# Delta rule, chunk stage: the folding's sums on TensorE instead of VectorE

## The reference, cut to what matters

```python
def step(S, inp):
    qt, kt, vt, at, bt = inp
    v_hat = jnp.einsum('bij,bi->bj', S, kt)
    err = vt - v_hat
    S = at[:, None, None] * S + bt[:, None, None] * (kt[:, :, None] * err[:, None, :])
    o = jnp.einsum('bij,bi->bj', S, qt)
    return (S, o)
_, O = lax.scan(step, S0, (Q.swapaxes(0, 1), Kh.swapaxes(0, 1), V.swapaxes(0, 1), alpha.T, beta.T))
```

## Time and profile before

| What | Value |
|---|---|
| Median of 3 runs (lowest to highest) | 4810.92 us (4806.46 to 4822.02) |
| The profiled execution's own time | 4811.17 us |
| Its span, first to last instruction | 4809.4 us |
| Busy over the span | PE 79%, DVE 81%, ACT 65%, POOL 37% |
| Chunk stage: first load issued to last record store issued | 485.3 to 758.1 us |
| From one unit's tables (L1973) to the next unit's, three times | 57.9, 57.0, 56.9 us |

### The profile page before, as it was taken

How to read it: one execution, slowest core, us unless ns; L and a number is a source line. 1 busy time by engine, 2 the same in 40 slices (tenths; PEclk the granted TensorE clock), 3 DMA queues, 4 the chain that set the end, 5 groups by cost and what they waited for, 6 DMA issues and landing times. The chain is left out here.

```text
span 4809.4 us, 64068 instructions
## 1 busy us (share of the span) xinstructions
PE 3801.0 (79%) x16142; PEld 1467.6 (31%) x16142; DVE 3888.0 (81%) x5877; ACT 3131.6 (65%) x4313; POOL 1799.2 (37%) x1796
## 2 busy tenths in 40 slices
PE   8986002656566988887689999999999999999488
PEld 3432001545453433342122222222222222222123
DVE  5536797999995655478789999999999999998344
ACT  5568101222222656447379999999999999999354
POOL 0000683666661001107434444444444444444112
PEclk9999556777778999999789999999999999999799
DMA  1013445444442000014511111111111111110300
GB/s 48 7 49 98 66 91 115 104 89 104 89 104 75 12 17 1 8 75 175 154 36 34 26 39 39 38 38 38 25 36 38 39 38 38 38 22 5 114 19 27
DMA packets 126458, 265.27 MB, mean 55 GB/s; under 512 B 41296, under 2 KB 70864, under 8 KB 117904
## 3 DMA queue, kind: packets, MB, share of 16 engines
q1 hardware_dynamic: 124208, 252.56, 22.1%
q10 hardware_dynamic: 1952, 9.18, 0.6%
HBM read 170.26 MB, written 91.26 MB: 54 GB/s over the span
## 5 line engine op out<-in xcount | busy, mean ns | idle before, releaser
L1241 POOL TENSOR_TENSOR att_heads_rest<-att_heads_probs,att_heads_high 128x352 f16<-128x352 f32 x1024 | 873.1, 853 | 1225.7 <-DVE att_heads_rest L1393 1165.8
L1373 DVE TENSOR_REDUCE att_heads_maxima<-att_heads_peek 128x1 f32<-128x1024 f32 x992 | 1208.1, 1218 | 26.1 <-PE att_heads_peek L1268 25.9
L1341 ACT ACTIVATE att_heads_probs<-att_heads_scores 128x1024 f32<-128x1024 f32 x1024 | 1057.0, 1032 | 153.7 <-PE att_heads_scores L1287 135.7
L1287 PE MATMUL att_heads_scores<-att_heads_q,att_heads_k 128*128 128x512 f16 (+1 forms) x4096 | 1071.8, 384 | 22.3 <-issue 18.9
L1343 ACT ACTIVATE att_heads_high<-att_heads_scores 128x1024 f16<-128x1024 f32 x1024 | 1053.5, 1029 | 0.0
L1393 DVE TENSOR_TENSOR att_heads_rest<-att_heads_probs,att_heads_high 128x672 f16<-128x672 f32 x1024 | 885.2, 864 | 66.1 <-POOL att_heads_rest L1241 54.7
L2112 PE MATMUL delta_scan_sums<-delta_scan_o_terms,main_identity 128*128 128x256 f32 x1536 | 406.7, 433 | 607.1 <-POOL delta_scan_o_terms L2180 607.1
L1268 PE MATMUL att_heads_peek<-att_heads_k,att_heads_q 112*128 112x512 f16 x1984 | 597.7, 382 | 17.3 <-DVE att_heads_maxima L1373 15.6
L2112 PEld LDWEIGHTS delta_scan_sums<-delta_scan_o_terms,main_identity 128*128 128x128 f32 x1536 | 336.7, 222 | 677.5 <-POOL delta_scan_o_terms L2180 620.3
L1287 PEld LDWEIGHTS att_heads_scores<-att_heads_q,att_heads_k 128*128 128x128 f16 (+1 forms) x4096 | 318.9, 98 | 693.1 <-issue 444.9
L1303 PE MATMUL att_heads_out<-att_heads_high,att_heads_v_head 128*64 128x512 f16 x2048 | 417.6, 404 | 15.8 <-DVE att_heads_rest L1393 15.2
(11 more groups left out here) (247 smaller groups left out, 4724.0 us busy)
## 6 DMA issues: line engine op xcount, KB each, us to landing
delta_scan_record<-delta_record SPq DMA_DIRECT2D x64, 898.0 KB, 9.5
att_heads_q<-att_hel SPq DMA_DIRECT2D x192, 128.0 KB, 3.0
att_heads_k<-att_hel SPq DMA_DIRECT2D x192, 128.0 KB, 3.2
att_hel<-att_hel_high SPq DMA_DIRECT2D x32, 512.0 KB, 4.5
att_hel<-att_hel_rest SPq DMA_DIRECT2D x32, 512.0 KB, 5.0
delta_record<-delta_chunks_record SPq DMA_DIRECT2D x64, 224.5 KB, 4.3
att_o<-att_heads_out_copy SPq DMA_DIRECT2D x256, 32.0 KB
att_out_parts<-att_o ACTq DMA_DIRECT2D x8, 1024.0 KB, 14.8
```

What stands on the lines that cost most here:

```text
L1241: nc.gpsimd.tensor_tensor(rest[:, step % 4, SPLIT:], probs[:, step % 4, SPLIT:], high[:, step % 4, SPLIT:], ALU.subtract).then_inc(rest_b_ ...
L1287: mm = nc.tensor.matmul(scores[:, step % 2, tokens(j)], k[0:rows, slot, number, tile * P:(tile + 1) * P], q[0:rows, slot, number, tokens(h ...
L1341: nc.scalar.activation(probs[:, step % 4], scores[:, step % 2], ACT.Exp, scale=LOGIT_SCALE).then_inc(probs_ready, 1)
L1373: nc.vector.tensor_reduce(maxima[:, m:m + 1], peek[:].rearrange("p j n -> p (j n)"), AX.X, ALU.max).then_inc(peek_read, 1)
```

## The change

In the first three of the four units, DVE no longer adds. `multiply` (new, in place of `fold`) does the same multiplication, but writes the products of column u into plane u of `fold_terms`: 384 neighbouring elements for each u, and so, for one chunk and row, 384 elements (1536 bytes) between one u and the next. PE adds the planes from s to 7 into one PSUM bank, `fold_sum`, by 8 - s matmuls of 384 columns with the identity as the other operand, and ACT copies the 384 sums into column s of the record. Two new semaphores chain them: `fold_summed` (PE to ACT) and `fold_placed` (ACT to DVE, PE and SP). `turn` of the unit after next is cut in two, k and q, and stands on ACT between the copies. The last unit is folded as before (`sum_fold` is the old `fold_sum`, renamed).

```diff
+        by_row = fold_terms[:].rearrange("p m r s -> p (m r s)").rearrange("p (s m r) -> p s m r", s=C, r=ROWS)
@@ sync, store(unit)
-                        sp.wait_ge(fold_step, unit * FOLDS + FOLDS * (run + 1 if len(runs_of(unit)) > 1 else 1))
+                        if unit + 1 < UNITS:
+                            sp.wait_ge(fold_placed, (unit + 1) * C)
+                        else:
+                            sp.wait_ge(fold_step, FOLDS * (run + 1))
@@ new: tensor
+                for unit in range(UNITS - 1):
+                    for s_row in range(C - 2, -1, -1):
+                        pe.wait_ge(fold_multiplied, unit * C + C - s_row)
+                        pe.wait_ge(fold_placed, unit * C + C - 1 - s_row)
+                        for u in range(s_row, C):
+                            mm = nc.tensor.matmul(fold_sum[:, 0:N * ROWS], c["identity"][:], by_row[:, u].rearrange("p m r -> p (m r)"),
+                                                  start=u == s_row, stop=u == C - 1)
+                        mm.then_inc(fold_summed, 1)
@@ scalar
+                turn(1)
                 for unit in range(UNITS):
-                    if unit + 1 < UNITS:
-                        turn(unit + 1)
...
+                    if unit + 1 == UNITS:
+                        continue
+                    for s_row in range(C - 2, -1, -1):
+                        act.wait_ge(fold_summed, unit * (C - 1) + C - 1 - s_row)
+                        nc.scalar.activation(folded(unit, slice(0, N))[:, :, :, s_row], fold_sum[:, 0:N * ROWS].rearrange("p (m r) -> p m r", r=ROWS),
+                                             ACT.Copy).then_inc(fold_placed, 1)
+                        if unit + 2 < UNITS and s_row in (3, 1):
+                            turn(unit + 2, 0 if s_row == 3 else 1)
@@ vector
+                def multiply(unit, s):
+                    last = s == C - 1
...
+                        dve.wait_ge(fold_placed, unit * C + C - 1 - s)
+                        dve.wait_ge(fold_multiplied, unit * C + C - 1 - s)
+                    whole = folded(unit, slice(0, N))
+                    out = whole[:, :, :, s:] if last else by_row[:, s:].rearrange("p s m r -> p m r s")
+                    ins = nc.vector.tensor_tensor(out, whole[:, :, :, s:], weights[:, :, s, s:].unsqueeze(2).broadcast_to([P, N, ROWS, C - s]), ALU.mult)
+                    ins.then_inc(fold_multiplied, 1)
...
+                    if more:
+                        for s in range(C - 1, -1, -1):
+                            multiply(unit, s)
+                            row_sum(unit + 1, 2 * (C - 1 - s))
+                            if s >= 1:
+                                row_sum(unit + 1, 2 * (C - 1 - s) + 1)
+                        continue
+                    dve.wait_ge(fold_placed, (UNITS - 1) * C)
```

More of the change, by code:

```diff
@@ L1789, in delta_chunks @@
         weights = s.ps("weights", [P, N, C, C])
+        fold_sum = s.ps("fold_sum", [P, BLK])
         k_loaded, q_loaded, ab_loaded = s.sem("k_loaded"), s.sem("q_loaded"), s.sem("ab_loaded")
@@ L1795, in delta_chunks @@
         decay_copied, in_ready = s.sem("decay_copied"), s.sem("in_ready")
+        fold_multiplied, fold_summed, fold_placed = s.sem("fold_multiplied"), s.sem("fold_summed"), s.sem("fold_placed")
         stored = [s.sem(f"stored{slot}") for slot in range(2)]
@@ L1864, in _ @@
                     sp.wait_ge(stored[slot], UNITS // 2 * RUNS * LOADS)
+            @block.tensor
+            def _(pe):
+                for unit in range(UNITS - 1):
[6 more added lines that the diff above has]
+                        mm.then_inc(fold_summed, 1)
             @block.gpsimd
@@ L1903, in _, with turn @@
             def _(act):
-                def turn(unit):
+                def turn(unit, only=None):
                     for w, loaded in enumerate((k_loaded, q_loaded)):
+                        if only is not None and w != only:
+                            continue
                         act.wait_ge(loaded, (unit + 1) * LOADS)
@@ L1977, in tables @@
                                             beta[:, :, 0:C - 1].unsqueeze(3).broadcast_to([P, N, C - 1, C - 1]), ALU.mult).then_inc(weights_ready, 1)
+                def multiply(unit, s):
+                    last = s == C - 1
+                    if last:
+                        dve.wait_ge(diagonal_ready, unit + 1)
+                        dve.wait_ge(mix_ready, unit + 1)
+                        dve.wait_ge(k_out_ready, unit + 1)
+                    else:
+                        dve.wait_ge(fold_placed, unit * C + C - 1 - s)
[4 more added lines that the diff above has]
+                    ins.then_inc(fold_multiplied, 1)
+                    if last:
+                        dve.wait_ge(fold_multiplied, unit * C + 1)
+                        dve.sem_inc(fold_placed, 1)
                 def fold(unit, run, s):
@@ L1983, in fold @@
                     last = s == C - 1
-                    before = (unit + run) * FOLDS + 2 * (C - 1 - s) - (0 if last else 1)
+                    before = run * FOLDS + 2 * (C - 1 - s) - (0 if last else 1)
                     if last:
@@ L1994, in fold, with sum_fold @@
                                             weights[:, chunks, s, s:].unsqueeze(2).broadcast_to([P, count, ROWS, C - s]), ALU.mult).then_inc(fold_step, 1)
-                def fold_sum(unit, run, s):
+                def sum_fold(unit, run, s):
                     chunks = runs_of(unit)[run]
-                    dve.wait_ge(fold_step, (unit + run) * FOLDS + 2 * (C - 1 - s))
+                    dve.wait_ge(fold_step, run * FOLDS + 2 * (C - 1 - s))
                     nc.vector.tensor_reduce(folded(unit, chunks)[:, :, :, s], fold_terms[:, chunks, :, s:], AX.X, ALU.add).then_inc(fold_step, 1)
@@ L2018, in _ @@
                             fold(unit, run, s)
-                            if more:
-                                row_sum(unit + 1, 2 * (C - 1 - s))
                             if s < C - 1:
-                                fold_sum(unit, run, s)
-                            if more and s >= 1:
-                                row_sum(unit + 1, 2 * (C - 1 - s) + 1)
+                                sum_fold(unit, run, s)
 def delta_recurrence(nc, c, dram, stage):
```

1 line of the change is left out of this document (added).

## The result

The changed kernel takes 4856.81 us (median of 4, 4851.16 to 4861.54) against 4808.69 for the kernel before on the same chip: a ratio of 1.0094, interval 1.0074 to 1.0114. Forecast was 4858.0. The profiled execution took 4860.4 us.

The account below looks back on a forecast made before the run. DVE set the pace before, POOL close behind; after the change, one trip DVE, PE, ACT bounds a unit: 72.6 us against 57.0, 15.6 more, three times. 4811.2 + 46.8 = 4858.0 us, range 4818 to 4876.

Parts of the forecast that it names:

- chain term: Folding of three units: one trip DVE, PE, ACT, DVE sets a unit, 72.6 us against 57.0, plus 46.8 us.
- The strides: DVE's seven multiplications a unit: writing 13,440 elements 1536 bytes apart costs 9.9 us more, ends 0 and 11.2.
- The full-clock part of the bursts: PE's sums in a unit at clock 1.00: 35 matmuls, 22.6 us, and start and drain, 1.8 us.
- the clock term: PE's bursts in a unit: each starts at clock 0.50 after its gap, 15.4 us more, ends 11.5 and 22.6.
- The last unit is unchanged: Fourth unit, folded as before: its time stays the same, priced at nothing.
- The covers: Work beside the chain priced at nothing: turn halves, last unit's loads (up to 8 us once if uncovered), DVE's unit end.
- The other cover: DVE's unit end: last row sum, tables, decays, 7.3 us, beside PE's last burst; uncovered, up to 1 us a unit.
- A: DVE's multiplications: strided writes are free, chain 62.7 us (down to 58.8), plus 5 to 17 us, 4822; chance 0.13.
- B: PE's bursts: clock stays at 1.00, strided writes pay; 57.2 us a unit, 4812, no change; chance 0.05.
- C: Folding: free writes and clock 1.00; POOL's floor of 51.3 us decides, minus 17 us, 4794; chance 0.04.
- D: PE's bursts: clock never warms, 79.8 us a unit, plus 68 us, 4880; chance 0.10.

Follow-up runs that it names:

- the run with the strides on DVE: Kernel before, with DVE writing the first three units' products in planes and its own sums reading them so: 4851.42 us, ratio 1.0076.
- the run with fillers: Changed kernel, with matmuls of 128 columns into a spare PSUM bank filling PE's gaps: 4824.05 us, ratio 1.0020.
- Halves: Changed kernel, each folding step in two halves of 8 chunks with own PSUM banks and semaphores: 4809.97 us, ratio 0.9981.
- The run without strides: Changed kernel, DVE writing contiguously and PE reading planes that don't hold the products (sums wrong, same work): 4828.18 us, ratio 1.0020.
- the run without strides and with fillers: Changed kernel, contiguous DVE writes and PE plane reads (sums wrong), plus matmuls of 128 columns in PE's gaps: 4809.84 us, ratio 0.9982.

## Why the prediction was right

The mechanism was right. That the time of 4858.0 lies 1.2 us from the median is luck in part: three errors nearly cancel, a chain term 3.2 us too large, 4.9 us in the stage that I had not counted, and a kernel before that stands at 4808.69 with its fourth execution, 2.5 below the 4811.2 that I started from. Nor could the times alone bear the forecast out so closely, as the ratio's interval is 36 to 55 us. The trace does.

**The chain term was too large**, 46.8 us forecast, 43.6 measured (periods 72.1, 71.7 and 71.6 against 57.9, 57.0 and 56.9). Term by term in the second unit: multiplications 25.4 (16.0 + 9.9 = 25.9 forecast); bursts 38.4 (22.6 + 1.8 + 15.4 = 39.8); copies 6.0 (5.7); diagonal 0.4 (0.3); the rest, the hand-overs, 1.4 (0.9). The sum is 71.6, where I had 72.6. The strides came out within 0.5 us (9.4 for 9.9), though the row that I took them from both reads and writes in steps, and reading costs something too, as the run with the strides on DVE shows: that the row's price fits writes alone was not to be expected. The full-clock part of the bursts is confirmed to 0.1 us by the run with fillers (24.45 against 24.4). So the clock term was the one mis-sized, 14.0 for 15.4, and within it the bursts of two to four matmuls: I had them at 0.50 throughout, 5.8 us more, and so, with start and drain, at 2.9, 4.2 and 5.4 us. They took 2.93, 3.73 and 4.42, together 4.5 us more than in the run with fillers: those of three and four matmuls had some of the clock back before their end (0.57 and 0.64 on average). The four longer ones lost 9.5 us together, as forecast from the output stage (9.6).

**"The last unit is unchanged" was wrong.** From its tables to DVE's last operation it takes 40.8 us, 3.8 more than the 37.0 before. Its first multiplication waits 4.13 us for the diagonal, which stands on ACT behind the third unit's last copy. I had this dependence in the chain of each changed unit, but it reaches into the fourth too, which I had priced at nothing; there the tables are the only thing beside the last burst, as no decays follow them. Halves shorten this wait to 0.95 us. The first unit's tables also stand 1.1 us later (542.2 for 541.1), as the whole stage does from its first load on, before anything that was changed. 43.6 + 3.8 + 1.1 = 48.5, which is what the last record store moved (758.1 to 806.6). All of the loss is in the stage, to within a microsecond of the 48.1 by the medians.

**The covers held**, with less to spare. The stores began at 620.4 and not at 613: I gave the first folding 67 us, but from its first multiplication (547.2) to the end of its last copy (620.3) it took 73.1, nearly all of the trip round the chain; the turn stood at 652.7 (650 forecast), and the load issued from 637.2 on was there. That left some 5 us, not 10, by the 10 us from issue to turn of the earlier trace rows. The other cover held too: with the last row sum, the tables and the decays done beside the last burst, DVE still waited 2.0 us for the diagonal. The halves of the turn cost the chain nothing, but they cost POOL 19.9 us of waiting, which I had not seen (6.8 us in the run with fillers, where the second half comes sooner).

**The rivals.** A, strided writes free: refuted by the 5.44 us for 3072 elements, and by the 25.35 us of a unit with PE idle. The run without strides shows what it would have been: 58.4 to 60.7 us a unit (58.8 to 62.7 forecast) and 9.6 us in all by its ratio (5 to 17 forecast). B, the clock held: it wasn't, and where fillers held it the second unit took 59.1 us and not 57.2: copies and multiplications cost 0.7 more than forecast and the rest, hand-overs, 1.1. C, both, as the run without strides and with fillers shows it: a real gain, but 53 us a unit and not 51.3, so 12.2 us in the three units where I gave it 17, and 8.7 by the ratio. D, never warm: the clock was 0.64 to 0.74, not 0.50.

Open: a diagonal copied ahead of the last column might take the last unit's 3.8 us away; it wasn't tried.

## What to carry to other kernels

Work that is taken off a busy engine is worth nothing if it comes back as a longer trip round a chain: count the trip, engine after engine, before counting busy time. A ring in which every engine waits for its neighbour can be mended by a second piece of work in it: halves took the waiting from 65.8 to 1.6 us with every step as dear as before. A layout serves the writer and the reader; where one wants rows and the other columns, groups of two f32 elements may please both.

## What the runs showed of the hardware

PE reading f32 columns in 32-byte steps takes 0.70 us for a record of 384 columns at granted clock 0.50 (4.51 less 3.12 us over 2 records) and 0.68 at 1.00 (9.81 less 3.00 over 10), 1.8 ns a column. Contiguous, it takes 0.64 us at 0.50 (4.21 less 2.93 over 2 records, the first unit's bursts of three and two matmuls) and 0.32 at 1.00 (4.78 less 1.56 over 10). So the steps cost PE 0.06 us a record at the slow clock and 0.36 at the full one: they take away what the clock would give back. In 8-byte steps PE is about 4% slower than in planes: bursts of 10 records of 192 columns take 1.97 against 1.89 us, both at 1.00. DVE pays 0.70 ns an element for writing single elements far apart (9.4 us for 13,440) and 0.61 for reading them (8.2 us).
